# Attention stacks folded into two row halves, scores and shifted scores sent to PE by turns

## The reference

```python
A1 = einsum('bhqd,bhkd->bhqk', Q1, K1) * scaling      # d = 8, 256 x 256
A2 = einsum('bhqd,bhkd->bhqk', Q2, K2) * scaling
A1 = where(causal, A1, -inf); A2 = where(causal, A2, -inf)
attn = softmax(A1) - lam[h] * softmax(A2)
O = einsum('bhqk,bhkd->bhqd', attn, V)                 # then RMS norm per head, and O @ Wo
```

## Time and profile before

| | |
|---|---|
| median of three runs | 471.52 us (471.31 to 473.81) |
| profiled execution, its own time | 472.45 us |
| its span, first to last instruction | 470.3 us |
| granted TensorE clock, mean over the span | 0.971 of full speed |
| PE busy | 407.5 us, 87% |
| PEld (weight loads, beside PE) busy | 265.0 us, 56% |
| DVE busy | 298.4 us, 63% |
| ACT busy | 262.5 us, 56% |
| POOL busy | 221.5 us, 47% |
| DMA | 34.48 MB, 45042 packets |

### The profile page before, as it was taken

How to read it: one execution, slowest core, us unless ns; L and a number is a source line. 1 busy time by engine, 2 the same in 40 slices (tenths; PEclk the granted TensorE clock), 3 DMA queues, 4 the chain that set the end, 5 groups by cost and what they waited for, 6 DMA issues and landing times.

```text
span 470.3 us, 9913 instructions
## 1 busy us (share of the span) xinstructions
PE 407.5 (87%) x3380; PEld 265.0 (56%) x3380; DVE 298.4 (63%) x1019; ACT 262.5 (56%) x631; POOL 221.5 (47%) x332
## 2 busy tenths in 40 slices
PE   0799589499999998989999899886689899999996
PEld 0665489455555555556555555533366666655574
DVE  6587264199878786887878688511133589999301
ACT  3433133105777676776767677687837643434842
POOL 9443032443447474563747456481300677774100
PEclk9999799958999999999999999999899999999999
DMA  8799969985555544145554410000000000000011
GB/s 208 238 293 299 247 155 253 120 92 72 70 70 69 70 64 66 25 60 69 70 71 57 66 21 3 2 4 0 1 1 1 1 0 2 0 1 1 0 47 45
DMA packets 45042, 34.48 MB, mean 73 GB/s; under 512 B 19265, under 2 KB 40897, under 8 KB 43457
## 3 DMA queue, kind: packets, MB, share of 16 engines
q1 hardware_dynamic: 44992, 33.86, 37.8%
HBM read 25.20 MB, written 8.39 MB: 71 GB/s over the span
## 4 chain that ended last, share of the span: by engine, by line
PE 58%; DVE 13%; ACT 10%; issue 7%; POOL 5%; DMA 4%; SPq 2%; POOLq 0%; DVEq 0%; ACTq 0%
PE ps L1009 7%; PE ps L1053 7%; PE ps L1030 5%; PE ps L1231 5%; PE ps L1057 4%; PE ps L657 3%; PE ps L1434 3%; PE ps L1012 3%; PE ps L1034 3%; DVE arena L1365 2%; PE ps L1004 2%; PE ps L1222 2%; DMA stack<-qk_parts 2%; PE ps L1100 2%; ACT arena L1175 2%
## 5 line engine op out<-in xcount | busy, mean ns | idle before, releaser
L833 ACT ACTIVATE arena<-ps 128x512 f32<-128x512 f32 x192 | 115.7, 606 | 51.7 <-PE ps L1030 29.0
L785 POOL TENSOR_SCALAR_AFFINE_SELECT arena<-arena 128x256 f32<-128x256 f32 (+1 forms) x192 | 90.7, 482 | 95.3 <-ACT arena L833 93.6
L961 DVE TENSOR_REDUCE arena<-ps 128x2 f32<-128x512 f32 x128 | 86.5, 688 | 13.6 <-PE ps L1012 13.5
L956 DVE CUSTOM_DVE_ANT_0 ps<-ps,future 128x128 f32<-128x128 f32 x256 | 66.6, 322 | 18.9 <-PE ps L1004 16.3
L1306 POOL TENSOR_TENSOR arena<-arena 128x1024 f32<-128x1024 f32 x16 | 34.2, 2135 | 33.9 <-DVE arena L1391 33.5
L1053 PE MATMUL ps<-arena 128*17 128x256 f32 x512 | 40.1, 385 | 0.0
L398 POOL TENSOR_TENSOR qk_parts_sb<-qk_rest,qk_parts_sb 128x512 bf16<-128x512 f32 x16 | 19.1, 1209 | 43.7 <-DVE qk_parts_sb L498 43.7
L1012 PE MATMUL ps<-future_bf,ident_bf 128*128 128x256 bf16 x128 | 37.0, 289 | 0.0
L956 DVE DVE_READ_ACCUMULATOR2_ANT arena<- 128x1 f32 x256 | 36.3, 142 | 0.0
L1434 PE MATMUL ps<-arena,upto 128*128 128x384 f32 x96 | 36.0, 487 | 0.0
L1231 PE MATMUL ps<-w,arena 128*128 128x128 f32 x256 | 31.2, 281 | 1.8 <-ACT arena L1198 1.3
(11 more groups left out here) (142 smaller groups left out, 811.8 us busy)
## 6 DMA issues: line engine op xcount, KB each, us to landing
qk_parts<-qk_parts_sb SPq DMA_DIRECT2D x16, 384.0 KB, 4.4
stack<-qk_parts SPq DMA_DIRECT2D x24, 256.0 KB, 6.5
arena<-qk_parts SPq DMA_DIRECT2D x24, 256.0 KB, 6.4
arena<-in_L_ffn_fc_B_dram SPq DMA_DIRECT2D x4, 1024.0 KB, 8.6
arena<-in_L_ffn_fc_A_dram SPq DMA_DIRECT2D x16, 256.0 KB, 4.6
xs<-in_L_attn_a_X_dram SPq DMA_DIRECT2D x4, 256.0 KB, 4.0
qk_parts<-qk_parts_sb SPq DMA_DIRECT2D x8, 128.0 KB, 4.4
out_dram<-xs SPq DMA_DIRECT2D x4, 256.0 KB, 2.4
```

The lines of the kernel that those rows point to most:

```text
L785: nc.gpsimd.affine_select(out=diag, in_=diag, compare_op=ALU.is_ge, fill=0.0, base=0, pattern=[[0, 2 if s < 2 else UMAPS], [1, P]], channe ...
L833: nc.scalar.activation(probs[:, r, s, :], ps[:, bank, :], ACT.Exp, scale=SCALE).then_inc(exp_done, 1)
L956: last = nc.vector.tensor_tensor_reduce(out=block, in0=block, in1=future[:], scale=1.0, scalar=LOWEST, op0=ALU.add, op1=ALU.max, accum_out ...
L961: last = nc.vector.tensor_reduce(out=rowmax[:, gs, 1, at:at + 2], in_=ps[:, bank, :].rearrange("p (m k) -> p m k", m=2), axis=AX, op=ALU.max)
```

## The change

The parts are:

1. **Stacks.** A stack keeps 48 rows of products and two of shift, no zeros between. Maps 0 to 7 of a group lie at partitions 0 to 49, maps 8 to 15 at 64 to 113 (`TILE_ROWS = 64`). So two units of a group use the lower half of the partitions, two the upper half. All four slots now lie in one tensor, `stacks`, outside the arena. Only the ones of k are filled, four fills in the first block, none in the second.
2. **Transfers.** `load_stack` issues six DMAs of half the size, `store_shift` four instead of two, with a semaphore for each half. The first two groups are loaded in the first block, after the stores of sequence 6 and before those of sequence 7; their loads come before SP's wait for the last stores.
3. **PE order.** Matmuls of the scores of unit j and of the shifted scores of unit j - 6, which always lie in opposite halves, are issued by turns (`both`). Before each such bank pair PE waits for both its score bank and its shifted bank to be free. The masks of banks 1 and 2 come at the end of the slot's products. The two parts of the value product are joined behind bank pair 0, the transpose of the maxima and the output projection come behind them.

```diff
-SROWS = 96
-XROWS = P
+TILE_ROWS = 64
+SROWS = TERMS * DH
+XROWS = SROWS + SHIFT_ROWS
...
+HMAPS = GMAPS // 2
...
-        stack01 = sb("stack01", [P, 2, 2, GMAPS, SEQ], BF16)
+        stacks = sb("stacks", [P, 4, 2, HMAPS, SEQ], BF16)
...
-        def fill_stacks(pool, slot, filled, before):
+        def fill_ones(slot, filled):
...
-            nc.gpsimd.memset(q, 0.0).then_inc(filled, 1)
+            k = stacks[:, slot, 1].rearrange("p m t -> p (m t)").bitcast(F32)
             nc.gpsimd.memset(k, pair).then_inc(filled, 1)
-            pool.wait_ge(filled, before + 2)
-            nc.gpsimd.memset(k[0:SROWS], 0.0).then_inc(filled, 1)
...
+                for h in range(2):
+                    src = bass.AP(whole.tensor, whole.offset + q_at * P * SEQ + h * HMAPS * SEQ,
+                                  [[row, 2 * DH], [(k_at - q_at) * P * SEQ, 2], [1, HMAPS * SEQ]])
+                    first = TILE_ROWS * h + 2 * DH * w
+                    eng.dma_start(stacks[first:first + 2 * DH, slot].rearrange("p s m t -> p s (m t)"), src)\
+                       .then_inc(stack_in[slot], 16)
...
+                    if b == 6:
+
+                        sp.wait_ge(parts_out[0], 48)
+                        sp.wait_ge(stacks_filled, 2)
+                        for g in range(2):
+                            load_stack(sp, g, g)
                 for u in range(2):
                     sp.wait_ge(parts_out[u], 48 * SEQS // 2)
-                sp.wait_ge(consts, 12)
-                for g in range(2):
-                    load_stack(sp, g, g)
...
+                for h in range(2):
+                    for part in range(SHIFT_ROWS):
+                        row = TILE_ROWS * h + SROWS + part
+                        sp.dma_start(stacks[row:row + 1, slot, 0],
+                                     shift[HMAPS * h:HMAPS * (h + 1), slot % 2, part, :])\
+                          .then_inc(shift_in[slot][h], 16)
...
+            def both(it, j, s):
+
+
+                scores_wait(it, j, s)
+                shifted_wait(it, j, s)
+                scores(it, j, s, 0)
+                shifted(it, j, s, 0)
+                scores(it, j, s, 1)
+                if s == 0:
+                    scores(it, j, s, 2)
+                shifted(it, j, s, 1)
+                if s == 0:
+                    scores(it, j, s, 3)
+                if s == 2:
+                    shifted(it, j, s, 2)
+                    shifted(it, j, s, 3)
...
             def emit(it, j):
-                for s in range(BANKS_U):
-                    if live(unit(it, j, 0), UNITS):
-                        score_bank(it, j, s)
-                    if live(unit(it, j, L_EXP), UNITS):
-                        shifted_bank(it, j, s)
...
+                both(it, j, 0)
+                if live(unit(it, j, L_PV), UNITS):
+                    for t in range(TPS):
+                        weigh_values(it, j, t)
+                g = group(it, j, L_SHIFT)
+                if (j - L_SHIFT) % UPG == 0 and live(g, GROUPS):
...
+                output_projection(it, j)
+                both(it, j, 1)
+                both(it, j, 2)
+                score_masks(it, j)
```

More of the change, by code:

```diff
@@ L81, in past @@
     return not isinstance(value, int) or value > 0
-def repeat(eng, turns, turn):
-    for it in range(turns):
-        turn(it)
 def hybrid_kernel(nc, X, Wq, Wk, Wv, Wo, lq1, lk1, lq2, lk2, rms_scale, bWq, bWk, bWv, bWo,
@@ L193, in halves, with stack_rows @@
             return ap.rearrange("p (h t) -> p h t", h=2)
[L195 to L203 removed]
+        def stack_rows(slot, side, half, n):
+            return stacks[TILE_ROWS * half:TILE_ROWS * half + n, slot, side]
         junk_columns = iter(range(16))
@@ L392, in _ @@
                 nc.gpsimd.memset(values[:, :, :, DV], 1.0)
-                for slot in range(2):
-                    fill_stacks(pool, slot, consts, 6 + 3 * slot)
+                for slot in range(4):
+                    fill_ones(slot, stacks_filled)
                 for b in range(SEQS):
@@ L740, in store_shift @@
                 sp.wait_ge(shift_lo, g + 1)
-                for part in range(SHIFT_ROWS):
-                    sp.dma_start(q_stack(slot)[SROWS + part:SROWS + part + 1], shift[:, slot % 2, part, :])\
-                      .then_inc(shift_in[slot], 16)
+                for h in range(2):
[4 more added lines that the diff above has]
+                          .then_inc(shift_in[slot][h], 16)
             store_shift(0, 0)
-            sp.wait_ge(filled_23, 6)
             load_stack(sp, 3, 3)
@@ L769, in attend_gpsimd @@
                 pool.sem_inc(started, FIRST)
-            for slot in (2, 3):
-                fill_stacks(pool, slot, filled_23, 3 * (slot - 2))
             def emit(it, j):
@@ L997, in score_bank, with scores @@
+            def scores(it, j, s, m):
+                if not live(unit(it, j, 0), UNITS):
+                    return
+                half, m0 = j % UPG // 2, UMAPS * (j % 2)
+                q, k = (stack_rows(j // UPG % 4, side, half, SROWS) for side in range(2))
                 bank = ps[:, S_BANK + s, :]
-                if s == 0 and j % UPG == 0:
-                    pe.wait_ge(stack_in[slot], 16 * len(WINDOWS) * (it + 1))
-                if past(n):
-                    pe.wait_ge(maxed, BANKS_U * (n - 1) + s + 1)
@@ new lines, in score_masks, with shifted_wait @@
+            def score_masks(it, j):
+                if live(unit(it, j, 0), UNITS):
+                    for s in range(1, BANKS_U):
+                        bank = ps[:, S_BANK + s, :]
+                        nc.tensor.matmul(bank.rearrange("p (m k) -> p m k", m=2)[:, :, P:SEQ], ident_bf[:],
+                                         future_bf[:], start=False, stop=True,
+                                         skip_group_check=True).then_inc(scored, 1)
+            def shifted_wait(it, j, s):
@@ L1019, in shifted_bank, with shifted @@
                 n = unit(it, j, L_EXP)
                 jj = j - L_EXP
-                slot, m0 = jj // UPG % 4, UMAPS * (jj % UPG)
-                q, k = q_stack(slot), k_stack(slot)
+                if live(n, UNITS):
+                    if s == 0 and jj % 2 == 0:
+                        pe.wait_ge(shift_in[jj // UPG % 4][jj % UPG // 2], 32 * (it + jj // SLOTS + 1))
+                    if past(BANKS_U * n + s - 1):
+                        pe.wait_ge(exp_done, BANKS_U * n + s - 1)
+            def shifted(it, j, s, m):
+                jj = j - L_EXP
+                if not live(unit(it, j, L_EXP), UNITS):
+                    return
+                half, m0 = jj % UPG // 2, UMAPS * (jj % 2)
+                q, k = (stack_rows(jj // UPG % 4, side, half, XROWS) for side in range(2))
```

95 lines of the change are left out of this document (37 added, 58 removed).

## The result

| | before | after |
|---|---|---|
| median, same comparison | 471.41 us (470.27 to 473.81) | 458.89 us |
| executions of after | | 455.39, 457.31, 460.48, 611.64 us |
| ratio | | 0.970 [0.962, 0.979] |
| profiled execution: its own time, span | 472.45, 470.3 us | 455.39, 453.3 us |
| mean granted clock in that span | 0.971 | 0.944 |

The change makes the kernel 3.0% faster: 14 us where 32 were forecast. The other three lie further apart (5 us) than those of before, and this turned out to be part of the answer.

A forecast was written before the change was run, and what follows sets the result against it. PE was taken to bound common attention slots. From 472.45 us, 29.4 for seven sequences and 2.5 at the start came off, giving 440.5; adjusted to the median of the runs, 439.5 us was forecast, range 430 to 461.

The forecast's parts named there:

- The sum by terms: PE's common attention slot: bank pairs, masks, transposes, value product and shape changes add to 2.22 us, against 2.81 before.
- the 0.15 allowed for coupling: Common slot: 0.15 us added because each bank pair waits for both DVE and ACT, giving 2.37; bounds zero and 0.4.
- pair 2: Third bank pair of a slot: shifted products start only after the second score product, so 640 columns, 0.27 us.
- no overlap: Rival: row halves do not run side by side, slot 2.87 us, time 460 (456 to 466); chance 0.12.
- a part eaten in common slots: Rival: halves overlap but loads, doubled waits or DVE make slots 2.6 us, time 452 (446 to 456); chance 0.22.
- the sequence sum: Eight attention slots plus maxima and once-a-sequence work: 23.4 us against 27.6, 29.4 us less over slots 8 to 63.
- the lack of slack: Common slot: DVE goes round in about PE's 2.2 us, its floor 2.16; ACT follows with 0.1 to 0.2 spare.
- SP issues twelve loads: Start: loads take 5 to 6 us ahead of the last stores; attention starts at 91.5, gaining 2.5 us.
- The 6.43 us of waiting for the stack: Start: PE's earlier wait for the first stack, taken as room against last stores landing after 94 us.
- a first product later than 94 us: Start of attention: sign that the forecast is wrong, because of the last stores; expected near 91.5 us.
- Slots 0 to 5 are DVE's, the last eight ACT's: no gain in either: Both ends of attention: other engines' floors, 2.16 us a slot for DVE and 2.03 for ACT, so no gain.
- The slower rival (the clock falls): Rival: PE stays at 1.2 GHz in attention, slot 4.0 us against 2.88, about 530 us; chance 0.09 including other overlap loss.

The follow-up runs named there:

- less work on DVE: Changed kernel with DVE's row maxima of score banks 1 and 2 taken over only the first 64 of 256 columns: 448.76 us, ratio 0.944.
- the later normalisation: Changed kernel with ACT's square and root and DVE's mean squares moved later in their slots: 456.24 us, ratio 0.963.
- head busy: Changed kernel with two unused full-array products of 256 columns added in each of slots 0 to 7: 456.78 us, ratio 0.967.
- after again: The changed kernel run again without an edit, for its spread: 455.98 us (450.99 to 458.89), ratio 0.965.
- start only: Changed kernel with only the first stack loaded ahead of the last stores, the second behind them: 451.12 us, ratio 0.947.
- with the tail kept busy, three kernels: Changed kernel with unused products in the eight slots after the last score: 453.02 us; also with second-stack loads behind the stores: 449.03; with all four edits: 448.64.
- the filler: Six unused full-array products of 256 columns ending each of the eight slots after the last score; alone on the changed kernel 453.02 us, ratio 0.963.
- old order: New stacks and transfers, but PE in the earlier kernel's order, nothing by turns, value product in two places: 552.86 us, ratio 1.125.
- the 48-row kernel: Kernel before the change, with score products contracting over 48 rows instead of 96 (the rest zeros): 498.81 us, ratio 1.059.

## Why the forecast was right and wrong

**The overlap, the changes of shape: right.** Bank pairs of 0.22 us, 0.11 us for each change, and the common slot of 2.28 to 2.32 us against 2.37. The sum by terms was 2.22; of the 0.15 allowed for coupling 0.06 to 0.10 was needed, and with less work on DVE it stayed, as a wait for ACT's exponential. One reason in the sum was wrong: pair 2 was put at 640 columns and 0.27 us, since its last shifted products would stand behind the second score product. It takes 0.22 like the others: the second shifted product starts at 215.98, ahead of that score product (216.02). The forecast also names L1009 after L1030 as the row where 96-row products follow 128-row ones at no cost; a value product stands between the two, and the rows that show it are L1030 after L1004 and L1012 after L1009, 0.22 and 0.23 us. The rivals of no overlap and of a part eaten in common slots fall. Slots with maxima gained more than forecast: 2.77 and 3.00 instead of 3.05.

The time itself, 458.89 us and 455.98 again, lies where the forecast had put no overlap (456 to 466) or a part eaten in common slots (446 to 456), and inside its range of 430 to 461. That is luck: neither mechanism happened.

**Work once a sequence: mis-sized, +1.5 us a sequence.** The step that failed most is the sequence sum, 8 x 2.37 + 2 x 0.68 + 3.1: it priced of the once-a-sequence work only what PE waited for or did before (2.7, grown to 3.1) and left every other engine's at nothing. Its cover was the 0.7 us a slot by which PE was the slowest, and the change takes just that away. What came out is 0.66 in slot 43 (POOL, then the square on ACT; moved away by the later normalisation, though half of it came back in slot 44) and 0.80 in slot 47 (DVE's statistics; gone with lighter maxima). The slots that went better give 0.6 back, so a sequence is 24.3 and not 23.4. The forecast had named the lack of slack, DVE 0 to 0.1 and ACT 0.1 to 0.2 us, and did not ask which instructions come only now and then. Of the 7.1 us missing in slots 8 to 63 some 6 are this, 0.9 a sequence; 1 is the disturbed sequence of slots 24 to 31. Single waits of this kind stand in some other traces too and not in all; their cause is open.

**The start: the right risk, a wrong price, 3.2 us.** The step "SP issues twelve loads (2.95 us for six, so 5 to 6 us)" became 6.9 us. But the larger mistake was to end the reckoning at the loads: the stores behind them were out only at 86.4, and the second block began near 94 whatever the stacks did. The 6.43 us of waiting for the stack was counted as room, while the whole chain (issue, landing, end of block) had moved into it. The forecast's own sign for this, a first product later than 94 us, came. Half of the loads behind the stores gives 4.1 us.

**The clock: taken for a rival of the whole of attention, when it acts at its ends.** "Slots 0 to 5 are DVE's, the last eight ACT's: no gain in either" held the clock as it was. In the first slots products and masks at 1.2 GHz end later than DVE wants them, +1.6 us; masks early gave 0.9 of it back at the same clock, so more than half is the masks' late place, and the rest was not split up. The clock came back at 116.7 us, beyond the 115 that the forecast had named as a sign. In the tail, from the last unit's scores to the end, the profiled executions took:

| | us | of these at clock 0.5, us |
|---|---|---|
| before | 171.2 | 3 |
| less work for DVE; masks early; value product split | 171.3, 171.9, 172.2 | 8, 7, 7 |
| after; head busy | 174.1, 173.9 | 17, 18 |
| normalisation later; after again; start only | 176.9, 177.3, 178.8 | 25, 27, 31 |
| with the tail kept busy, three kernels | 172.1, 172.0, 171.9 | 5, 3, 3 |

Five of eight profiled executions without the filler lost 2 to 8 us here (old order and the 48-row kernel aside), and three of three with it lost under 1. The loss grows with the time at 0.5, and the times of one kernel go with their mean clocks (451 to 459 us in the changed kernel). So the low clock in the tail goes with most of the spread that the traces can show. Of the two faster executions with the start alone, 9 us ahead of the slower two, there is no trace. What makes the clock fall in one execution and not in the next is not shown. Nor is it shown why one execution of the changed kernel had a mean of 0.563.

**Where the gain went, in short:** the overlap gives what it should in each slot; of the 15 us missing in the profiled execution, 3 are the stores behind the loads, some 6 work on other engines that had been hidden, 1 a single wait, 3 the clock in the tail, and 1.6 the first slots, by late masks and a slow PE together. The start's 3 can be had back by an order of transfers, and with the tail at full clock the kernel is at 449 us.

**What the alternation itself is worth** is larger than the whole gain: in the old order the new stacks are 12% slower than before even by the two fastest executions, and not 3% faster. At full clock their common slot is 3.32 us, 0.44 more than before, so the clock is not the whole of it. The slower rival (the clock falls) describes that kernel, its median 82 us over before, but not by its sum: a common slot at 1.2 GHz takes 5.5 us there and not 4.0.

## What to carry to other kernels

When the slowest engine is made a fifth faster, list for each other engine the instructions that come only once in several slots, and add them to that engine's slot; the average slack says nothing on them. When a transfer is moved ahead in a queue, follow what was behind it to its landing and to whoever stands at the end of the block. Halving the rows of a product pays only if the other half works at the same moment: each change of array shape costs, and without the overlap the clock did not hold here.

## What the runs showed of the hardware

- Products in two row halves, with partitions from 0 and from 64, run wholly side by side: both start within 0.01 us and 2 x 512 columns take 0.22 to 0.23 us at 2.4 GHz, with a weight load for each product. A product of one half started 0.04 us ahead of a product of the other half that stands before it in the program (pair 2). The scores' 48 and the shifted scores' 50 rows share a shape.
- A change between half-row and full-row products costs 0.10 to 0.11 us, as one to column strips does. That agrees with the Trainium skill, "TensorEngine Tiling (Array Packing)", Key Properties: a change of mode drains TensorE.
- PE recorded busy 12.00 of 12.00 us was granted 1.2 GHz in one stretch and 2.4 GHz in another of the same execution, with the same program. With half-row products issued one after the other (old order) the low level held for 150 us on end, with the same products by turns the high one came at 116.7 us in after and stayed to the end of the scores.
